# Cross-attention probabilities made by key instead of transposed, in a fused decoder layer

## The chip, the cores and the metric

One core of a Trainium2 chip runs the whole kernel. The metric is the device time of one execution in microseconds.

## The reference

A decoder layer over 32 independent batches of 112 tokens of width 256. The change touches only the cross-attention to 375 context positions, 16 heads of width 16:

```python
x = layernorm(x + self_attention_with_threshold(x, W))
q, k, v = heads(x @ Wq + bq), heads(ctx @ Wk + bk), heads(ctx @ Wv + bv)
scores = einsum('bhqd,bhkd->bhqk', q, k) / 4
scores = where(mask, -1e15, scores)            # mask depends on batch and key
attn = softmax(scores)                         # over the 375 keys
x = layernorm(x + einsum('bhqk,bhkd->bhqd', attn, v) @ Wo + bo)
x = layernorm(x + mixture_of_2_of_8_experts(x))
```

## The kernel before

All engines run one loop over iterations, and each iteration works on five batches at once, one per stage: in iteration `it` the stage "self" (self-attention) handles batch it+2, "proj" (q, k and v) it+1, "attn" (cross-attention scores to weighted values) it, "join" (output projection, second layer norm, gating) it-1, "moe" it-2. An iteration is cut into 20 slots (`SLOTS`). Every engine has its own in-order program that goes through the slots 0 to 19, and the engines meet only at semaphores. `USES` says in which slot TensorE makes each product of the other stages and in which PSUM bank (G0 to G2 or O); before a product, TensorE waits until the bank's previous product has been taken.

Batch a's cross-attention before: `scores(a, n)` on TensorE makes the 112 x 375 scores of one head as one fp32r matmul (q and k are split in a high and a low part, stacked on 96 partitions in `q_stack` and `k_stack`, which SP's DMA queue fills with 24 transfers a batch). The sign is turned, so the most negative value is the maximum. `head` on VectorE (L595) adds the mask, writes `masked` and gives the least value as `nmax`. `exponent` on ScalarE (L475) makes `probs` with `nmax` as bias and sums them. `transpose_probs` (L920) transposes them in three pieces into PSUM, ScalarE (L505) copies them to `probsT`, and `weigh_values` (L936) multiplies four heads at a time by the values into bank O. In the next iteration ScalarE copies the result to `o_sb` (L490), TensorE transposes the widened reciprocals (`rb`, L993), and VectorE multiplies them (`attnT`, L649) ahead of `Wo` (L1000).

Order within a slot on TensorE: first a score, then the transposes of an earlier head, then the slot's products, then, in slots 7, 11, 15 and 19, the weighing of values. Scores 0 and 1 of the next batch are in slots 18 and 19. Other names: `x1T`, `qT` (L968), `K0`, `K1` (L979), `V0` to `V2` (L986) are proj's products, `m0` to `m3` (L1042) the experts' (six fp32r matmuls of 512 columns each), `Sc`, `PT`, `att` self's, `x2T` and `lg` (L1030, L1033) join's. ScalarE takes `x1T` first in slot 0 (L484), `q_sb` in slot 3, `k_hi` (L528) in 4 and 7, `self_exp` (L519) in 6. SP's loop is: load x, context and mask, store the output, wait for `q_lo` from VectorE (slot 5), 12 transfers to `q_stack` (L386), 12 to `k_stack` (L395).

## Time and profile before

| what | us |
|---|---|
| median of 3 runs (868.3 to 870.01) | 868.95 |
| profiled execution, its own time | 868.0 |
| its span | 866.2 |
| TensorE busy | 829.0 (96%) |
| VectorE busy | 723.7 (84%) |
| ScalarE busy | 650.5 (75%) |
| GpSimd busy | 199.7 (23%) |

Matmul records overlap, since they are pipelined; busy time is the union of an engine's records. A line number names the instruction's line in the kernel before.

### The profile page before, as it was taken

To read this page: it belongs to the slowest core of one execution; us is meant where nothing else is said; L and a number is where in the kernel's file an instruction comes from. 1 tells how busy PE (TensorE), PEld (TensorE's weight loads), DVE (VectorE), ACT (ScalarE), POOL (GpSimd) and SP (SyncE) were. 2 spreads that over 40 slices of the span, in tenths; PEclk is the share of its full clock that TensorE was granted. 3 is DMA by queue.
4 is the path that set the end of the run, shared out by engine and by line. 5 is a ranking of instruction groups with operands and counts; after the bars stand their busy time and mean duration, and the time that the engine had idled before them with its cause. 6 is when DMAs were issued, how large, how long until landed. Compare 5 with 4: busy or idle time off the path is not lost.

```text
span 866.2 us, 25528 instructions
## 1 busy us (share of the span) xinstructions
PE 829.0 (96%) x7844; PEld 723.8 (84%) x7844; DVE 723.7 (84%) x2836; ACT 650.5 (75%) x1961; POOL 199.7 (23%) x293
## 2 busy tenths in 40 slices
PE   4789999999999999999999999999999999999985
PEld 3678888888888888888888888888888888888863
DVE  3547888888998888888988898998888998888765
ACT  2458877788887777888877788887777888777760
POOL 2202122222222222222222212222222222222101
PEclk9999999999999999999999999999999999999999
DMA  8634444443434444433444433444444333433300
GB/s 261 163 98 104 114 108 109 123 114 86 104 98 111 109 115 117 95 98 96 113 109 110 123 94 101 100 106 106 113 118 103 99 100 100 108 86 84 92 8 11
DMA packets 89830, 91.08 MB, mean 105 GB/s; under 512 B 19440, under 2 KB 85600, under 8 KB 89696
## 3 DMA queue, kind: packets, MB, share of 16 engines
q1 hardware_dynamic: 89696, 89.45, 41.0%
q8 instruction: 65, 1.06, 0.5%
q14 instruction: 69, 0.57, 0.2%
HBM read 26.84 MB, written 3.67 MB: 35 GB/s over the span
## 4 chain that ended last, share of the span: by engine, by line
PE 87%; DVE 3%; SPq 3%; DMA 2%; issue 2%; ACT 1%; POOL 1%; DVEq 0%; POOLq 0%; ACTq 0%
PE psum L1042 19%; PE psum L920 18%; PE psum L911 11%; PE psum L936 10%; PE psum L986 8%; PE psum L979 7%; PE psum L968 3%; PE psum L1000 3%; SPq L386 2%; SPq L395 1%; PE psum L957 1%; DVE mix L609 1%; PE psum L950 1%; PE psum L962 1%; DMA wout_sb<-in_wout 1%
## 5 line engine op out<-in xcount | busy, mean ns | idle before, releaser
L475 ACT ACTIVATE probs<-masked,nmax 112x375 f32<-112x375 f32 x512 | 312.9, 611 | 77.6 <-DVE nmax L595 76.6
L595 DVE CUSTOM_DVE_ANT_0 masked<-psum,mask_add 112x375 f32<-112x375 f32 x512 | 276.6, 541 | 53.7 <-PE psum L911 42.8
L505 ACT ACTIVATE probsT<-psum 125x336 f32<-125x336 f32 x512 | 228.6, 447 | 63.2 <-PE psum L920 58.3
L920 PE MATMUL psum<-const_sb,probs 112*125 112x112 f32 x1536 | 251.1, 272 | 0.1
L920 PEld LDWEIGHTS psum<-const_sb,probs 112*125 112x125 f32 x1536 | 235.8, 188 | 16.0 <-issue 6.8
L911 PE MATMUL psum<-k_stack,q_stack 96*112 96x376 f32 x512 | 203.4, 397 | 3.3 <-DMA k_stack<-k_hi 2.7
L418 POOL TENSOR_SCALAR var_eps<-moments 112x1 f32<-112x1 f32 x96 | 21.2, 220 | 485.6 <-DVE moments L699 191.1
L609 DVE SCALAR_TENSOR_TENSOR mix<-psum,gate,mix 112x256 f32<-112x256 f32 x224 | 107.7, 481 | 14.6 <-PE psum L1042 1.3
L1042 PE MATMUL psum<-we_hi,x_hi 128*112 128x512 f32 x256 | 108.0, 422 | 2.4 <-DVE mix L609 2.4
L911 PEld LDWEIGHTS psum<-k_stack,q_stack 96*112 96x112 f32 x512 | 90.1, 176 | 22.5 <-issue 13.4
L1042 PE MATMUL psum<-we_hi,x_lo 128*112 128x512 f32 x256 | 100.8, 394 | 0.0
L936 PE MATMUL psum<-probsT,v_sb 125*32 125x112 f32 x3072 | 100.1, 263 | 0.5 <-ACT probsT L505 0.5
L1042 PE MATMUL psum<-we_lo,x_hi 128*112 128x512 f32 x256 | 100.4, 392 | 0.0
L475 ACT ACTIVATION_READ_ACCUMULATOR probs<-masked,nmax 112x1 f32 x512 | 100.1, 196 | 0.0
L936 PEld LDWEIGHTS psum<-probsT,v_sb 125*32 125x32 f32 x3072 | 69.2, 109 | 19.5 <-issue 6.3
L452 POOL TENSOR_TENSOR ctx_lo<-ctx_sb,ctx_hi 128x752 fp32r<-128x752 f32 x32 | 57.9, 1809 | 118.3 <-DVE vac_scaled L739 107.4
L986 PE MATMUL psum<-wv_hi,ctx_hi 128*125 128x256 f32 x192 | 59.9, 312 | 1.5 <-DVE we_lo L577 0.9
L1042 PEld LDWEIGHTS psum<-we_hi,x_lo 128*112 128x112 f32 x256 | 44.7, 175 | 14.7
L422 POOL TENSOR_TENSOR rstd<-var_eps,minus_half 112x1 f32<-112x1 f32 x96 | 54.7, 569 | 8.0
L986 PE MATMUL psum<-wv_lo,ctx_hi 128*125 128x256 f32 x192 | 53.8, 280 | 0.0
L1042 PEld LDWEIGHTS psum<-we_hi,x_hi 128*112 128x112 f32 x256 | 45.0, 176 | 10.6 <-DVE mix L609 3.2
L986 PE MATMUL psum<-wv_hi,ctx_lo 128*125 128x256 f32 x192 | 53.8, 280 | 0.0
...
## 6 DMA issues: line engine op xcount, KB each, us to landing
k_stack<-k_hi SPq DMA_DIRECT2D x256, 93.8 KB, 2.2
q_stack<-q_hi SPq DMA_DIRECT2D x256, 56.0 KB, 2.0
...
k_stack<-k_lo SPq DMA_DIRECT2D x128, 93.8 KB, 2.2
q_stack<-q_lo SPq DMA_DIRECT2D x128, 56.0 KB, 2.0
...
```

Of the source, the lines that this page charges most:

```text
L422: nc.gpsimd.tensor_tensor(rstd[n - 1][:, :], var_eps[n - 1][:, :], minus_half[:, :], ALU.pow)\
L452: nc.gpsimd.tensor_tensor(ctx_lo[k][:, :, :], ctx_sb[k][:, :, :], ctx_hi[k][:, :, :].bitcast(fp32), ALU.subtract)\
L475: nc.scalar.activation(probs[:, n % RING, :], masked[:, n % RING, :], ACT.Exp, bias=nmax[:, n:n + 1], scale=-1.0, accum_out=probs_sum[a[1] ...
L505: nc.scalar.activation(probsT[:, i % TRING, :], psum[0:KP, T_BANKS[i % 2], 0:KT * TOK], ACT.Copy).then_inc(probsT_copied, 1)
L595: nc.vector.tensor_tensor_reduce(masked[:, n % RING, :], psum[0:TOK, S_BANKS[n % 2], 0:KEYS], mask_add[k][:, :], 1.0, 3.0e38, ALU.add, ALU ...
L609: nc.vector.scalar_tensor_tensor(out=mix[:, :], in0=bank_of[f"m{e // 2}"][0:TOK, (e % 2) * DIM:(e % 2 + 1) * DIM], scalar=gate[k][:, e:e + ...
L911: nc.tensor.matmul(psum[0:TOK, S_BANKS[n % 2], 0:KEYS_EVEN], q_stack[k][:, c, pair, odd, :], k_stack[k][:, c, pair, :], start=True, stop=T ...
L920: mm = nc.tensor.transpose(psum[0:KP, T_BANKS[n % 2], j * TOK:(j + 1) * TOK], probs[:, n % RING, j * KP:(j + 1) * KP], ident[0:TOK, 0:TOK])
L936: mm = nc.tensor.matmul(o_bank[32 * j:32 * j + 32, c * TOK:(c + 1) * TOK], v_sb[k][:, t, pair, odd:odd + 2, :].rearrange("p e d -> p (e d) ...
L979: mm = nc.tensor.matmul(bank[:, 0:KEYS_EVEN], w_part[:, c, r * 128:(r + 1) * 128], x_part[:, c, :], start=(n == 0), stop=(n == 3 * DC - 1))
L986: mm = nc.tensor.matmul(bank[0:KP, 0:DIM], x_part[:, c, j * KP:(j + 1) * KP], w_part[:, c, :], start=(n == 0), stop=(n == 3 * DC - 1))
L1042: mm = nc.tensor.matmul(bank[0:TOK, 0:width], x_part[:, c, :], w_part[:, c, :], start=(n == 0), stop=(n == len(parts) - 1))
```

## The change

The cross-attention is split over two stages and the scores are made twice. In "attn" (batch it) TensorE still makes the scores by query and VectorE still takes the least value, but only that value is used. After eight heads TensorE transposes the eight columns (`mx0`, `mx1`), ScalarE copies them negated into `nmaxT`, and SP sends them through a scratch tensor in DRAM to partition 96 of `q_stack`, whose partner row in `k_stack` is all ones. In the new stage "heads" (batch it-1) there are 12 blocks: ScalarE lays the mask of 125 keys by 4 x 112 queries into PSUM (`lay_mask`), TensorE adds two fp32r matmuls of 97 rows on top (`score_block`), and ScalarE's exponential writes the transposed probabilities at once (`exponent`). The values have a 17th column of ones, which gives the sum of the probabilities. The result is copied (`o_sb`), transposed to queries (`oT`), divided by VectorE (`rden`, `o_norm`), and transposed back (`aT`). "join" and "moe" move one iteration later, so that the loop has one iteration more. `q_stack`, `k_stack` and `v_sb` have three buffers, the mask has four. ScalarE's `ctx_hi` moves from slot 1 to slot 12, `V0` from 9 to 10.

```diff
+BLOCKS = QUADS * KT
+STACKS = 3
+MASKS = 4
...
-S_BANKS, T_BANKS, O_BANK, G_BANKS = (0, 1), (2, 3), 4, (5, 6, 7)
...
-USES = [("x1T", 0, "G2"), ("m0", 1, "G1"), ("rb", 1, "O"), ("qT", 2, "G2"), ("K0", 3, "G0"), ("Wo", 4, "G1"), ("Sc", 5, "G2"),
-        ("K1", 6, "G1"), ("m1", 8, "G0"), ("V0", 9, "G2"), ("x2T", 10, "G1"), ("PT", 11, "G0"),
-        ("m2", 12, "G2"), ("att", 13, "G1"), ("lg", 14, "G0"), ("V1", 15, "G2"), ("m3", 16, "G1"),
-        ("V2", 18, "G0")]
+S_BANKS, ST_BANKS, O_BANK, G_BANKS = (0, 1), (2, 3), 4, (5, 6, 7)
+USES = [("x1T", 0, "G2"), ("m0", 1, "G1"), ("aT", 1, "G0"), ("qT", 2, "G2"), ("K0", 3, "G0"), ("Wo", 4, "G1"),
+        ("Sc", 5, "G2"), ("K1", 6, "G1"), ("m1", 8, "G0"), ("mx0", 8, "G2"), ("V0", 10, "G2"), ("x2T", 10, "G1"),
+        ("PT", 11, "G0"), ("m2", 12, "G2"), ("att", 13, "G1"), ("lg", 14, "G0"), ("V1", 15, "G2"), ("oT", 15, "O"),
+        ("m3", 16, "G1"), ("mx1", 16, "G0"), ("V2", 18, "G0")]
...
-          "attn": (0, ()),
-          "join": (-1, ("rb", "Wo", "x2T", "lg")),
-          "moe": (-2, ("m0", "m1", "m2", "m3")),
+          "attn": (0, ("mx0", "mx1")),
+          "heads": (-1, ("oT",)),
+          "join": (-2, ("aT", "Wo", "x2T", "lg")),
+          "moe": (-3, ("m0", "m1", "m2", "m3")),
...
-FIRST, LAST = -2, BATCH + 2
+FIRST, LAST = -2, BATCH + 3
...
+            def neg_max_to_scratch(at, c):
+                sp.wait_ge(act_attn.sem, act_attn.to(f"nmaxT{c}", at))
...
+                sp.dma_start(neg_max_scratch[c], nmaxT[c][:, :].bitcast(fp32)).then_inc(neg_max_out[c], 16)
+            def neg_max_to_stack(at, c):
...
+                sp.wait_ge(neg_max_out[c], 16 * (at[1] + 1))
+                settle(sp)
+                sp.dma_start(q_stack[b][96:97, c, :, :, :].rearrange("o p h q -> o (p h q)").bitcast(fp32),
+                             neg_max_scratch[c].rearrange("(o h) q -> o (h q)", o=1)).then_inc(neg_max_in[b][c], 16)
...
+                if heads:
+                    neg_max_to_scratch(w, 1)
...
+                if heads:
+                    neg_max_to_stack(w, 1)
...
+                if attn:
+                    neg_max_to_scratch(a, 0)
...
+                        if n == 2 and attn:
+                            neg_max_to_stack(a, 0)
...
+                def lay_mask(w, i):
+                    b = w[1] % MASKS
+                    if i == 0:
+                        act.wait_ge(mask_in[b], turn(w, 1, MASKS))
+                        if w[1] == 0:
+                            act.wait_ge(setup_pe, 2)
+                    if due(count(w, BLOCKS, i - 1)):
+                        act.wait_ge(probs_ready, count(w, BLOCKS, i - 1))
+                    t = i % KT
+                    nc.scalar.activation(
+                        psum[0:KP, ST_BANKS[i % 2], 0:4 * TOK].rearrange("p (h q) -> p h q", h=4),
+                        mask_u8[b][:, KEYS + t * TOK:KEYS + (t + 1) * TOK].unsqueeze(1).broadcast_to([KP, 4, TOK]),
+                        ACT.Copy, scale=BIG).then_inc(mask_laid, 1)
+                def exponent(i):
+                    group, t = i // KT, i % KT
+                    act.wait_ge(blocks_ready, count(w, BLOCKS, i + 1))
+                    if t == 0 and due(count(w, QUADS, group - 1)):
+                        act.wait_ge(pv_done, count(w, QUADS, group - 1))
+                    nc.scalar.activation(probsT[:, group % 2, t, :], psum[0:KP, ST_BANKS[i % 2], 0:4 * TOK],
+                                         ACT.Exp, scale=-1.0).then_inc(probs_ready, 1)
...
+                    if heads and n < BLOCKS:
+                        exponent(n)
+                        if n + 2 < BLOCKS:
+                            lay_mask(w, n + 2)
+                    if n >= SLOTS - 2 and active("heads", it + 1):
+                        lay_mask(a, n - (SLOTS - 2))
+                    if join and n == 2:
+                        act.wait_ge(pe_join.sem, pe_join.to("aT", o))
+                        nc.scalar.activation(attnT[:, :], bank_of["aT"][:, 0:DC * TOK], ACT.Copy)\
+                          .then_inc(act_join.did("attnT"), 1)
+                    if attn and n in (9, 17):
+                        c = (n - 9) // 8
+                        act.wait_ge(pe_attn.sem, pe_attn.to(f"mx{c}", a))
+                        if due(16 * a[1]):
+                            act.wait_ge(neg_max_out[c], 16 * a[1])
+                        nc.scalar.activation(nmaxT[c][:, :], bank_of[f"mx{c}"][0:CHUNK_HEADS, 0:TOK],
+                                             ACT.Copy, scale=-1.0).then_inc(act_attn.did(f"nmaxT{c}"), 1)
...
+                    if heads and n == 14:
+                        act.wait_ge(pv_done, count(w, QUADS, QUADS))
+                        nc.scalar.activation(o_sb[:, :], o_bank[:, 0:QUADS * TOK], ACT.Copy)\
+                          .then_inc(act_heads.did("o_sb"), 1)
+                    if own and n == 12:
                         act.wait_ge(ctx_in[k], turn(s, 1))
...
+            for k in range(STACKS):
+                nc.vector.memset(v_sb[k][:, :, :, HEAD_DIM:HEAD_DIM + 1], 1.0)
+                nc.vector.memset(k_stack[k][0:96, :, :, KEYS:KEYS_EVEN].bitcast(fp32), 0.0)
+                nc.vector.memset(k_stack[k][96:97, :, :, :].bitcast(fp32), 1.0)
+            nc.vector.memset(o_bank[:, 0:QUADS * TOK], 0.0)
             nc.vector.memset(ones[:, :], 1.0).then_inc(setup_dve, 1)
...
                     nc.vector.tensor_tensor_reduce(
-                        masked[:, n % RING, :], psum[0:TOK, S_BANKS[n % 2], 0:KEYS],
+                        scores_left[:, n % 2, :], psum[0:TOK, S_BANKS[n % 2], 0:KEYS],
                         mask_add[k][:, :], 1.0, 3.0e38, ALU.add, ALU.min,
-                        nmax[:, n:n + 1]).then_inc(masked_ready, 1)
+                        nmax[:, h:h + 1]).then_inc(max_ready, 1)
...
+                            by_head = o_bank[0:TOK, :].rearrange("q (h r) -> q h r", h=HEADS)
+                            nc.vector.reciprocal(rden[:, :, :], by_head[:, :, HEAD_DIM:HEAD_DIM + 1])\
+                              .then_inc(dve_heads.did("rden"), 1)
+                            dve.wait_ge(dve_heads.sem, dve_heads.to("rden", w))
+                            nc.vector.tensor_tensor(
+                                o_norm[:, :, :], by_head[:, :, 0:HEAD_DIM],
+                                rden[:, :, :].broadcast_to([TOK, HEADS, HEAD_DIM]), ALU.mult)\
+                              .then_inc(dve_heads.did("o_norm"), 1)
...
+            def open_blocks():
+                for bank in ST_BANKS:
+                    for j in range(4):
+                        mm = nc.tensor.matmul(psum[:, bank, j * TOK:(j + 1) * TOK], ident, ident[:, 0:TOK],
+                                              start=(j == 0), stop=True, skip_group_check=True)
...
+                def score_block(w, i):
+                    b, group, t = w[1] % STACKS, i // KT, i % KT
+                    c = group // 2
+                    if i % (BLOCKS // DC) == 0:
+                        pe.wait_ge(neg_max_in[b][c], turn(w, 1, STACKS))
+                    pe.wait_ge(mask_laid, count(w, BLOCKS, i + 1))
+                    for e in range(2):
+                        pair = 2 * (group % 2) + e
+                        mm = nc.tensor.matmul(psum[0:KP, ST_BANKS[i % 2], 2 * e * TOK:2 * (e + 1) * TOK],
+                                              k_stack[b][:, c, pair, t * KP:(t + 1) * KP],
+                                              q_stack[b][:, c, pair, :, :].rearrange("p h q -> p (h q)"),
+                                              start=False, stop=True, skip_group_check=True)
+                    mm.then_inc(blocks_ready, 1)
+                def weigh_values(group):
...
+                    pe.wait_ge(probs_ready, count(w, BLOCKS, KT * group + KT))
+                    if group == 0:
+                        pe.wait_ge(dve_proj.sem, dve_proj.to("v2", w))
+                        if due(dve_heads.to("o_norm", o)):
...
+                            pe.wait_ge(dve_heads.sem, dve_heads.to("o_norm", o))
                     for t in range(KT):
                         for j in range(4):
-                            pair = 4 * c + j
                             mm = nc.tensor.matmul(
-                                o_bank[32 * j:32 * j + 32, c * TOK:(c + 1) * TOK],
-                                v_sb[k][:, t, pair, odd:odd + 2, :].rearrange("p e d -> p (e d)"),
-                                probsT[:, (4 * quad + j) % TRING, t * TOK:(t + 1) * TOK],
-                                start=(odd == 0 and t == 0), stop=(odd == 1 and t == KT - 1),
+                                o_bank[32 * j:32 * j + HEAD_DIM + 1, group * TOK:(group + 1) * TOK],
+                                v_sb[w[1] % STACKS][:, t, 4 * group + j, :],
+                                probsT[:, group % 2, t, j * TOK:(j + 1) * TOK],
...
                                 tile_position=(0, 32 * j), skip_group_check=True)
                     mm.then_inc(pv_done, 1)
...
                                                   w_part[:, c, :], start=(n == 0), stop=(n == 3 * DC - 1))
-                    elif name == "rb":
-                        pe.wait_ge(dve_attn.sem, dve_attn.to("rden_wide", o))
-                        pe.wait_ge(act_join.sem, act_join.to("o_sb", o))
+                    elif name in ("mx0", "mx1"):
+                        c = int(name[2])
+                        pe.wait_ge(max_ready, count(a, HEADS, CHUNK_HEADS * (c + 1)))
+                        mm = nc.tensor.transpose(bank[0:CHUNK_HEADS, 0:TOK],
+                                                 nmax[:, CHUNK_HEADS * c:CHUNK_HEADS * (c + 1)], ident[0:TOK, 0:TOK])
+                    elif name == "oT":
+                        pe.wait_ge(act_heads.sem, act_heads.to("o_sb", w))
+                        for g in range(QUADS):
+                            mm = nc.tensor.transpose(bank[0:TOK, g * 128:(g + 1) * 128],
+                                                     o_sb[:, g * TOK:(g + 1) * TOK], ident)
+                    elif name == "aT":
+                        pe.wait_ge(dve_heads.sem, dve_heads.to("o_norm", o))
                         for c in range(DC):
                             mm = nc.tensor.transpose(
...
-                    if attn and 2 <= n < HEADS + 2:
-                        transpose_probs(n - 2)
+                    if heads and n < BLOCKS - 1:
+                        score_block(w, n + 1)
+                    if n == SLOTS - 1 and active("heads", it + 1):
+                        score_block(a, 0)
                     for u, (name, slot, _) in enumerate(ALL_USES):
...
+                        open_blocks()
+                    if heads and n >= 4 and (n - 4) % 3 == 0 and n <= 13:
+                        weigh_values((n - 4) // 3)
                 if it == FIRST:
```

## Rows read from the trace of the kernel before

**Rows 1.** The page: busy time of each engine.

```profile
PE 829.0 (96%) x7844; PEld 723.8 (84%) x7844; DVE 723.7 (84%) x2836; ACT 650.5 (75%) x1961; POOL 199.7 (23%) x293
```

**Rows 2.** Windows, one iteration: length, PE, PEld, DVE, ACT, POOL busy, clock, DMA.

```profile
420.13:445.08 24.95, 24.95 (x244) 22.02 (x243) 22.24 (x88) 20.14 (x62) 6.16 (x10) 1.00 0.43 109
```

**Rows 3.** Chain of one iteration: shares, then pieces (start, us, line).

```profile
by line: PE psum L1042 22.3%; PE psum L920 21.5%; PE psum L911 12.6%; PE psum L936 11.4%; PE psum L986 9.1%; PE psum L979 8.3%; PE psum L968 3.6%; PE psum L1000 3.5%; PE psum L957 1.7%; PE psum L950 1.6%; PE psum L962 1.4%; PE psum L993 0.8
...
420.29 0.20 PE psum L993 x2
...
437.30 0.10 PE psum L1033
...
443.68 0.17 PE psum L911
443.85 1.40 PE psum L1042 x6
```

**Rows 4.** Groups by form, ScalarE: shapes, count, busy us and mean ns, idle before.

```profile
L475 ACT ACTIVATE probs<-masked,nmax 112x375 f32<-112x375 f32 x512 | 312.9, 611 | 77.6 <-DVE nmax L595 76.6
...
L505 ACT ACTIVATE probsT<-psum 125x336 f32<-125x336 f32 x512 | 228.6, 447 | 63.2 <-PE psum L920 58.3
...
L528 ACT ACTIVATE k_hi<-psum,bk_col 128x375 fp32r<-128x375 f32 x64 | 36.2, 566 | 2.0 <-PE psum L979 2.0
...
L484 ACT ACTIVATE x1T<-psum 128x224 f32<-128x224 f32 x32 | 11.2, 351 | 7.1 <-PE psum L962 6.8
```

**Rows 5.** Timeline of ScalarE at slot 0: start, duration.

```profile
443.72 0.36 ACT L484 ACTIVATE x1T<-psum 128x224 f32<-128x224 f32 x1
443.97 0.35 ACT L490 ACTIVATE o_sb<-psum 128x224 f32<-128x224 f32 x1
```

**Rows 6.** Timeline of TensorE: slot 0's x1T, slot 2's score 3.

```profile
443.27 0.41 PE L962 MATMUL psum<-const_sb,x 112*128 112x112 f32 x2
...
445.21 0.40 PE L911 MATMUL psum<-k_stack,q_stack 96*112 96x376 f32 x1
```

**Rows 7.** Timeline of VectorE: the end of head 1, then out_sb.

```profile
444.88 0.08 DVE L595 DVE_READ_ACCUMULATOR2_ANT nmax<- 112x1 f32 x1
445.48 0.41 DVE L642 TENSOR_SCALAR out_sb<-mix,moments,rstd 112x256 f32<-112x256 f32 x1 [0.52 <-POOL rstd L422]
```

**Rows 8.** Waits from 100 to 796 us: total, times, longest.

```profile
DVE masked L595 <- PE psum L911: 21.3, 48, 0.6
```

**Rows 9.** SP's queue: timeline, and the issues' time to landing.

```profile
450.41 0.59 SPq L386 DMA_DIRECT2D q_stack<-q_hi  x1
...
550.72 1.25 SPq L386 DMA_DIRECT2D q_stack<-q_hi  x2
...
566.71 1.27 SPq L395 DMA_DIRECT2D k_stack<-k_hi  x1
...
k_stack<-k_hi SPq DMA_DIRECT2D x256, 93.8 KB, 2.2
```

**Rows 10.** Timelines of VectorE and ScalarE at the start.

```profile
1.33 0.38 DVE L561 MEMSET v_sb<- 125x384 f32 x1
...
1.73 0.15 DVE L563 MEMSET ones<- 128x112 f32 x1
...
7.71 0.34 ACT L519 ACTIVATE self_exp<-psum,self_nmax 112x112 f32<-112x112 f32 x1
```

**Rows 11.** Timeline of TensorE: rb in iterations 2, 30, 31 and 32.

```profile
94.89 0.35 PE L993 MATMUL psum<-const_sb,rden_wide 112*128 112x112 f32 x2
...
796.02 0.36 PE L993 MATMUL psum<-const_sb,rden_wide 112*128 112x112 f32 x2
...
820.61 0.36 PE L993 MATMUL psum<-const_sb,rden_wide 112*128 112x112 f32 x2
...
841.59 0.36 PE L993 MATMUL psum<-const_sb,rden_wide 112*128 112x112 f32 x2
```

**Rows 12.** Windows of 2 us, TensorE in the drain: busy, clock, DMA.

```profile
852.00:854.00 2.00, 0.10 (x1) 1.00 0.00 0
```

284 lines of the change are left out of this document (123 added, 161 removed).

## The prediction

> **What bounds the kernel now.** I read the page first: TensorE is busy for 96% of the span [rows 1]. Then the windows view over exactly one turn of the loop, from one set of rb transposes to the next: 24.95 us, of which TensorE is busy for all, VectorE for 22.24, ScalarE for 20.14, at a granted clock of 1.00, which is 2.4 GHz [rows 2]. So TensorE sets the pace and VectorE is close behind. The chain through that turn is TensorE alone, and its shares say what each product costs [rows 3]: the transposes of the probabilities (L920) 21.5%, or 5.36 us; the scores (L911) 12.6%; m0 to m3 (L1042) 1.40 each; K (8.3%) 1.04 each; V (9.1%) 0.72 each; qT 0.89; Wo 0.87; weigh_values (11.4%) 0.71 each. The average turn over 28 of them is (796.02 - 94.89) / 28 = 25.04 us [rows 11], 0.09 above that clean turn.
>
> What the average hides is the order. TensorE, ScalarE and VectorE each walk through 20 slots in program order, and the question for each new hand-over is what stands in front of it.
>
> **TensorE's own work.** Removed: 5.36 us. Added: 12 blocks of two fp32r matmuls, 125 columns loaded and 224 streamed. In the chain, fp32r products pay by columns: 512 cost 1.40 / 6 = 0.233, 376 cost 0.17 [rows 3]. The slope puts 224 at 0.10, and one that streams only 8 still costs 0.10 (L1033) [rows 3], a floor for loading. So 0.105 each, 0.21 a block, 2.52 a turn. oT is four transposes, each 0.10 like those of rb (0.20 for two), 0.42 with the change of mode after it; mx0 and mx1 one each, 0.17 with it. aT replaces rb at the same price; weigh_values has as many matmuls as before. Sum: 24.95 - 5.36 + 2.52 + 0.42 + 0.34 = 22.87, call it 22.9 us. If that were all, the turn would be 2.05 us shorter.
>
> **ScalarE's own work.** Removed: 16 x (611 + 447) ns = 16.9 us of records (L475, L505) [rows 4], and the reads of the accumulator. Added: 12 exponentials and 12 masks of 448 columns. From 224 to 336 columns a copy grows from 351 to 447 ns, 0.857 ns a column [rows 4]. The exponential: 611 + 73 x 0.857 = 674 ns by L475, 566 + 63 = 629 by L528, which also reads PSUM; I take 0.65. The mask: 447 + 96 = 543 by L505; no row writes PSUM or reads bytes, so 0.45 to 0.60, and I take 0.56. In total 14.5 us, so ScalarE's busy time falls by some 3 us. The Trainium skill ("ScalarE: Activation LUTs", section What ACT_TABLE_LOAD costs) gives 280 ns + 0.833 a column with a pointer for the bias and 186 ns without: the first would be 0.65 for the exponential, the second 0.56 for it and for the mask; by the second the turn below would be 24.55 and the run some 6 us shorter. Where the two differ, L475 (611) lies nearer the first.
>
> **The new wait.** lay_mask(n+2) waits for exponent(n), the instruction just ahead of it, so these two don't overlap. And TensorE's block 2 stands in slot 1, ahead of m0, and needs lay_mask(2), which ScalarE issues in slot 0 behind x1T's copy and exponent(0). x1T's copy needs TensorE's slot 0. From the start of x1T on TensorE: 0.41 until its end [rows 6], 0.04 hand-over (443.68 to 443.72) [rows 5, 6], 0.25 from one copy to the next [rows 5], 0.65, 0.04, 0.56, 0.04: block 2 starts at 1.99. TensorE has only x1T (0.20, as rb) and one score (0.17) [rows 3] before it. It stands for 1.6 us, each turn, with nothing that could cover it, for m0 is queued behind.
>
> From there ScalarE needs 0.65 + 0.04 + 0.56 - 0.10 = 1.15 a slot, nine slots 10.35, plus attnT 0.25 and q_sb's two copies 0.5 [rows 5], two k_hi 0.92 (566 ns less 0.1 of overlap [rows 4]), self_exp 0.34 [rows 10]: lay_mask(11) is done at 1.95 + 12.35 = 14.3. TensorE's slots 1 to 9 and the first score of slot 10 are 12.6 us (m0, aT, qT, K0, Wo, Sc, K1, m1, mx0, two weigh_values, scores and blocks): 14.6. So ScalarE keeps up barely, and I add 0.2. The turn is 22.9 + 1.6 + 0.2 = 24.7 us, with the 0.09 on top [rows 11] 24.8: a gain of 0.25 a turn, over 28 turns 7 us.
>
> **VectorE.** It loses a reciprocal, a widening copy and attnT and gains a reciprocal and a multiply of 256 columns (0.41 by out_sb [rows 7]): about even. Its head 1 ends at 444.96 and TensorE's score 3 starts at 445.21 [rows 6, 7]: 0.25 apart, and out_sb then waits 0.52 for POOL [rows 7]. In 28 turns it waits 21.3 us for scores, 0.76 a turn [rows 8]: without these, a turn of its own is 24.95 - 0.76 = 24.2. It doesn't set the pace at 24.8, but a faster TensorE would find it at 24.2 (and 22.24 if all its gaps were waits [rows 2]). TensorE's new pause in slot 1 gives it that time. So even if ScalarE's price were much lower, little more than 1 us a turn could be won.
>
> **SP's queue.** From score 3 (445.21) to the first q_stack issue (450.41) is 5.2 us, from there to the last k_stack issue 16.0 (550.72 to 566.71), landing 2.2 [rows 6, 9]: 23.4 us round, with score 3 of the next turn waiting at its end. Into this come neg_max_to_scratch(a, 0) and neg_max_to_stack(a, 0). A q_stack issue takes 0.59 [rows 9], and these have far fewer rows; two add 0.7 to 1.2 with their waits, and 0.3 goes with the transposes: 23.8 to 24.3. Covered by the turn of 24.7, by half a microsecond. The other two go into SP's idle time. The first half of the maxima is on its way some 2 us before block 0 needs it; the second leaves once out_dram has been issued, lands 2.2 us later, and block 6 is in slot 5: about 1 us to spare. ctx_hi's move and x1_bo's third buffer cost nothing; POOL has the time.
>
> **What is paid once.** (a) The pipeline is one stage deeper. The iteration inserted near the end has no attn and no proj: 12 x 1.15 + 1.0 on ScalarE, then oT and o_norm, 16.3 us. The one before it took 20.98 us (820.61 to 841.59) [rows 11] and falls to 22.9 - 6.4 (its missing products by the shares) [rows 3] + 1.6 = 18.1. Net +13.4. (b) Three memsets of one partition by 3008 elements: v_sb's 384 elements took 378 ns, 112 took 152 [rows 10], 0.83 ns an element, so 2.56 us each; with o_bank's VectorE is free at 9.9 us instead of 1.9, and self_exp, at 7.71 before [rows 10], starts at 10.35. open_blocks adds eight fp32 matmuls ahead of att. Together 3.5 us (bounds 1 and 6). (c) Two issues more in the first turn, where SP's queue is what is waited for: 1. Sum 17.9.
>
> **The sum.** The profiled execution took 868.0 us, its span 866.2; the median of the runs is 868.95, 0.95 higher. 868.0 - 7 + 17.9 = 878.9, as a median 880. A turn of 24.3 is the break-even point.
>
> **Rivals.**
> 1. Faster: ScalarE's pair is nearer 0.95 us, the pause of TensorE shrinks, and VectorE's 24.1 is the turn; with once-costs of 14: 28 x (24.1 + 0.09 - 25.04) = -24, so 859. For it: the unknown price of a write into PSUM. Against: 0.41 + 0.25 + 0.61 in the chain of the pause are rows. 0.17.
> 2. The change does all it says (22.9 a turn): 868.95 - 58 + 18 = 829. Against it VectorE's 24.2. 0.04.
> 3. Slower by more: a wait on the ScalarE or DMA path costs another 0.9 us, turn 25.6 (ScalarE's self-wait 0.1 dearer each time makes its nine slots 1 us longer; or the maxima for block 6 land late): 868.95 + 18 + 18 = 905. It decides once SP's loop passes 24.7 or ScalarE's slot 1.2 us. 0.14.
> 4. fp32r at 224 columns runs at the rate of fp32. Wo's two matmuls of 256 columns take 0.87 (3.5%) [rows 3], so 224 would take 0.38: 24 x 0.275 = 6.6 us a turn, some 1075 in all. No fp32r product of the trace streams between 17 and 255 columns. 0.08.
> 5. The pause lowers TensorE's clock. In the drain it stayed at 1.00 in a window with 0.10 us of work out of 2 [rows 12]. If m0, qT and K0 ran at half rate: 3.3 us a turn, 975. 0.03.
> The forecast's own case, turns of 24.4 to 25.1, 869 to 891: 0.54.
>
> **How the numbers follow.** No change within 0.2% (1.7 us, about what a measurement can tell) takes 0.06 from the lower edge of the forecast's case. Faster: rivals 1 and 2, 0.21. Slower: the rest, 0.73. The range 858 to 905 leaves out rivals 2, 4 and 5 and the tails of the others, some 0.18.
>
> **What would show it.** In the trace after: the block matmuls 0.105 apart (rival 4 if 0.38); TensorE idle some 1.6 us ahead of block 2 in slot 1, released by ScalarE's mask, 32 times; mask 0.56, exponential 0.65; VectorE's waits for scores not much smaller; score 3 not waiting for k_stack; block 6 not waiting for q_stack; three memsets of 2.56 at the start; one more iteration of 16 us at the end. The prediction is wrong if the pause is under 1 us or the turn is outside 24.4 to 25.1.

## The result, and the profile after

The changed kernel takes 919.68 us (median of four runs, 918.96 to 923.61) against 869.13 for the kernel before: a ratio of 1.059, with a 95% interval of 1.056 to 1.062. The forecast was 880 with a range of 858 to 905. The sign was right; the size was short by 40 us, and the time lies outside the range.

The page of the changed kernel, its busy row and the row of TensorE's granted clock in 40 slices. TensorE's busy time fell from 829.0 us [rows 1] to 809.1, ScalarE's from 650.5 to 558.6, and the run still became longer.

```profile
PE 809.1 (88%) x7284; PEld 662.8 (72%) x7284; DVE 750.5 (82%) x2810; ACT 558.6 (61%) x1289; POOL 200.3 (22%) x293
...
PEclk9888799999999999999999999999999999999998
```

The same page's groups: shapes, count, busy us and mean ns, idle before. These are the three new instructions. The two of ScalarE cost less than forecast: exponential 0.536 (0.65 forecast), mask 0.543 (0.56). The third is the block's matmul; its 281 ns are the length of a record and not what it adds to TensorE's work, which is read further down from start to start.

```profile
L524 ACT ACTIVATE probsT<-psum 125x448 f32<-125x448 f32 x384 | 205.9, 536 | 24.3 <-PE psum L982 22.8
L513 ACT ACTIVATE psum<-mask_u 125x448 f32<-125x448 uint8 x384 | 206.8, 543 | 10.1
L982 PE MATMUL psum<-q_stack,k_stack 97*125 97x224 f32 x768 | 147.8, 281 | 13.5 <-ACT psum L513 12.3
```

Where the time went is read from the same instruction in each iteration. Timelines of TensorE: x1T of the iterations -1, 2 and 30, then aT of the iterations 31, 32 and 33.

```profile
21.72 0.61 PE L1024 MATMUL psum<-const_sb,x 112*128 112x112 f32 x2 [3.00 <-DVE x L855]
...
100.62 0.39 PE L1024 MATMUL psum<-const_sb,x 112*128 112x112 f32 x1
...
825.38 0.36 PE L1024 MATMUL psum<-const_sb,x 112*128 112x112 f32 x2
...
853.00 0.35 PE L1063 MATMUL psum<-const_sb,o_norm 112*128 112x112 f32 x2
...
874.38 0.36 PE L1063 MATMUL psum<-const_sb,o_norm 112*128 112x112 f32 x2
...
892.47 0.35 PE L1063 MATMUL psum<-const_sb,o_norm 112*128 112x112 f32 x2
```

In the kernel before, x1T stood at 92.35 in iteration 2 and at 794.20 in iteration 30, and its span was 866.2. So the 51.7 us between the spans are:

| stretch | before | after | difference | forecast |
|---|---|---|---|---|
| to x1T of iteration 2 | 92.35 | 100.62 | +8.3 | +4.5 |
| 28 turns | 25.07 each | 25.88 each | +22.9 | -7 |
| from there to the end | 72.0 | 92.5 | +20.5 | +13.4 |

The forecast's differences add up to 10.9 us, so 40.8 us of the 51.7 are the miss, and three quarters of it (29.9) are the turn. The mean of 25.88 holds two early turns, of the iterations 2 and 3, that took 26.10 and 28.09; all the others but one take 25.75 to 25.81. One turn after, in windows (length, PE, PEld, DVE, ACT, POOL busy, clock): TensorE is idle for 1.85 us of it, at a clock of 1.00, and VectorE is busy for 22.85 us where it was busy for 22.24 [rows 2].

```profile
438.35:464.16 25.81, 23.96 (x228) 19.78 (x227) 22.85 (x88) 17.23 (x40) 6.19 (x9) 1.00 0.42 106
```

The waits of TensorE, then of VectorE, from 200 to 700 us, which is 19.4 turns (total, times, longest). The mask (L513) that the forecast had made responsible for 1.6 us a turn is named for 0.26; VectorE is named for 1.45, in two places.

```profile
PE psum L968 <- DVE nmax L652: 16.2, 20, 0.8
PE psum L1048 <- DVE mix L666: 11.9, 20, 0.6
PE psum L982 <- ACT psum L513: 5.1, 20, 0.3
PE psum L1048 <- ACT nmaxT L550: 3.4, 20, 0.2
...
DVE scores_left L652 <- PE psum L968: 16.9, 47, 0.7
DVE out_sb L699 <- POOL rstd L456: 11.0, 20, 0.6
DVE x L855 <- POOL rstd L456: 8.0, 20, 0.4
```

The pause itself, in the timelines of TensorE, ScalarE and VectorE. From x1T to block 2 it is 1.82 us (1.99 forecast). But a first part of it, 0.82 us, is score 2 waiting for VectorE's head 0, and only then comes 0.24 for the mask. Head 0 ends at 439.38, and score 2 stands between it and block 2, so that by this chain block 2 could start 0.24 us before it does; the mask ends at 440.12.

```profile
438.35 0.36 PE L1024 MATMUL psum<-const_sb,x 112*128 112x112 f32 x2
439.53 0.40 PE L968 MATMUL psum<-k_stack,q_stack 96*112 96x376 f32 x1 [0.82 <-DVE nmax L652]
440.17 0.47 PE L982 MATMUL psum<-q_stack,k_stack 97*125 97x224 f32 x2 [0.24 <-ACT psum L513]
...
438.75 0.36 ACT L532 ACTIVATE x1T<-psum 128x224 f32<-128x224 f32 x1 [0.98 <-PE psum L1024]
439.00 0.54 ACT L524 ACTIVATE probsT<-psum 125x448 f32<-125x448 f32 x1
439.57 0.55 ACT L513 ACTIVATE psum<-mask_u 125x448 f32<-125x448 uint8 x1
...
439.30 0.08 DVE L652 DVE_READ_ACCUMULATOR2_ANT nmax<- 112x1 f32 x1
```

### The profile page after: what moved, and what is told of

Its sections match the earlier page's. It is cut to its first block, busy times and chain, and to the rows that moved or that the text cites. A ratio compares the mean times of both kernels' runs of the same rounds, so it can differ in the third digit from the quotient of the medians.

```text
span 917.9 us, 22878 instructions
## 1 busy us (share of the span) xinstructions
PE 809.1 (88%) x7284; PEld 662.8 (72%) x7284; DVE 750.5 (82%) x2810; ACT 558.6 (61%) x1289; POOL 200.3 (22%) x293
## 4 chain that ended last, share of the span: by engine, by line
PE 56%; DVE 21%; issue 10%; ACT 5%; SPq 5%; DMA 2%; POOL 0%; DVEq 0%; POOLq 0%; ACTq 0%
PE psum L1112 11%; PE psum L982 8%; DVE scores_left L652 7%; PE psum L1041 7%; PE psum L968 7%; PE psum L1048 6%; PE psum L998 5%; DVE mix L666 5%; PE psum L1030 3%; PE psum L1070 3%; SPq L413 2%; ACT psum L513 2%; ACT probsT L524 2%; SPq L427 2%; PE psum L1058 1%
## 5 line engine op out<-in xcount | busy, mean ns | idle before, releaser
L652 DVE CUSTOM_DVE_ANT_0 scores_left<-psum,mask_add 112x375 f32<-112x375 f32 x512 | 275.3, 543 | 70.9 <-PE psum L968 62.9
L968 PE MATMUL psum<-k_stack,q_stack 96*112 96x376 f32 x512 | 197.4, 394 | 32.0 <-DVE nmax L652 25.0
L524 ACT ACTIVATE probsT<-psum 125x448 f32<-125x448 f32 x384 | 205.9, 536 | 24.3 <-PE psum L982 22.8
L513 ACT ACTIVATE psum<-mask_u 125x448 f32<-125x448 uint8 x384 | 206.8, 543 | 10.1
L982 PE MATMUL psum<-q_stack,k_stack 97*125 97x224 f32 x768 | 147.8, 281 | 13.5 <-ACT psum L513 12.3
L982 PEld LDWEIGHTS psum<-q_stack,k_stack 97*125 97x125 f32 x768 | 131.8, 191 | 25.9 <-ACT psum L513 22.8
L666 DVE SCALAR_TENSOR_TENSOR mix<-psum,gate,mix 112x256 f32<-112x256 f32 x224 | 107.4, 479 | 18.1 <-PE psum L1112 6.0
L998 PE MATMUL psum<-probsT,v_sb 125*17 125x112 f32 x3072 | 98.5, 261 | 0.0
L998 PEld LDWEIGHTS psum<-probsT,v_sb 125*17 125x17 f32 x3072 | 66.0, 97 | 30.0 <-issue 21.0
L1048 PE MATMUL psum<-wv_hi,ctx_hi 128*125 128x256 f32 x192 | 60.7, 316 | 22.9 <-DVE mix L666 16.9
L555 ACT ACTIVATE o_sb<-psum 128x448 f32<-128x448 f32 x32 | 17.4, 544 | 77.1 <-PE psum L998 77.1
L1048 PEld LDWEIGHTS psum<-wv_hi,ctx_hi 128*125 128x125 f32 x192 | 35.6, 186 | 33.3 <-DVE mix L666 19.4
```

The costliest lines, as they stand in the source:

```text
L513: nc.scalar.activation(psum[0:KP, ST_BANKS[i % 2], 0:4 * TOK].rearrange("p (h q) -> p h q", h=4), mask_u8[b][:, KEYS + t * TOK:KEYS + (t + ...
L524: nc.scalar.activation(probsT[:, group % 2, t, :], psum[0:KP, ST_BANKS[i % 2], 0:4 * TOK], ACT.Exp, scale=-1.0).then_inc(probs_ready, 1)
L652: nc.vector.tensor_tensor_reduce(scores_left[:, n % 2, :], psum[0:TOK, S_BANKS[n % 2], 0:KEYS], mask_add[k][:, :], 1.0, 3.0e38, ALU.add, A ...
L666: nc.vector.scalar_tensor_tensor(out=mix[:, :], in0=bank_of[f"m{e // 2}"][0:TOK, (e % 2) * DIM:(e % 2 + 1) * DIM], scalar=gate[1 - k][:, e ...
L968: nc.tensor.matmul(psum[0:TOK, S_BANKS[n % 2], 0:KEYS_EVEN], q_stack[b][0:96, c, pair, odd, :], k_stack[b][0:96, c, pair, :], start=True, ...
L982: mm = nc.tensor.matmul(psum[0:KP, ST_BANKS[i % 2], 2 * e * TOK:2 * (e + 1) * TOK], k_stack[b][:, c, pair, t * KP:(t + 1) * KP], q_stack[b ...
```

## The experiments

"Turn" below is the mean of ten iterations in the middle, from x1T of iteration 10 to that of iteration 20: 25.06 before, 25.78 after. "Theory A" is the forecast's own, "B" that VectorE sets the pace, "B2" that two chains end together in slot 1, "C" that the memsets and `open_blocks` make the start longer, and "D" that SP's queue holds the turn up. Ratios are against the kernel before.

| run | median us | ratio, 95% interval | turn |
|---|---|---|---|
| e1: mask first | 907.25 | 1.045 (1.039 to 1.051) | 25.33 |
| e2: ctx_lo after x_cas | 902.98 | 1.040 (1.034 to 1.045) | 25.19 |
| e3: head 0 first | 920.61 | 1.059 (1.053 to 1.064) | 25.79 |
| e4: start | 913.89 | 1.052 (1.047 to 1.057) | 25.82 |
| e5: e1 and e3 | 908.49 | 1.046 (1.043 to 1.049) | 25.31 |
| e6: e5 and e2 | 894.21 | 1.029 (1.023 to 1.036) | 24.81 |
| e7: e6 and e4 | 887.25 | 1.022 (1.019 to 1.025) | 24.78 |
| e8: e7, maxima by ScalarE's queue | 885.94 | 1.022 (1.017 to 1.026) | 24.84 |
| e9: e8, mask early | 878.13 | 1.012 (1.008 to 1.016) | 24.80 |
| e10: e9, o_norm last | 887.76 | 1.023 (1.019 to 1.027) | 25.04 |
| e11: e9, no wait for GpSimd | 870.44 | 1.001 (0.999 to 1.003) | 24.45 |
| e12: e11, k by ScalarE's queue | 866.87 | 0.997 (0.996 to 0.998) | 24.47 |
| e13: ctx_hi back | 905.35 | 1.043 (1.039 to 1.047) | 25.29 |
| e14: m3 light | 939.67 | 1.080 (1.074 to 1.085) | 26.55 |
| e15: m1 light | 920.41 | 1.059 (1.054 to 1.064) | 25.79 |

**One part at a time.**

e1, on ScalarE:

```diff
+                    if heads and n == 0:
+                        exponent(0)
+                        lay_mask(w, 2)
                     if proj and n == 0:
...
-                    if heads and n < BLOCKS:
+                    if heads and 0 < n < BLOCKS:
```

> ScalarE takes exponent(0) and lay_mask(2) ahead of the copy of x1T in slot 0, so that block 2 finds its mask laid. Theory A (the prediction's: ScalarE's hand-over in slot 1 is what TensorE stands for, and its pause sets the turn): the whole pause of some 1.06 us between x1T and block 2 goes, the turn falls from 25.8 to 24.8, the run from 920 to about 890. Theory B (each turn has two parts, one paced by TensorE up to score 9, one paced by VectorE from its head 9 to head 0 of the next batch; the pause waits for VectorE's head 0, then only 0.24 us for the mask): only the 0.24 us of the mask go, 28 x 0.24 = 7 us, 913, and score 2 still waits 0.8 us for VectorE.

It gave 0.45 us a turn: neither the whole pause nor the 0.24 alone, so both figures missed. Why it is more than the 0.24 isn't shown. The waits of TensorE in this run no longer name the mask, and score 2 waits for head 0 as long as before (16.3 us, 20 times).

e2, on GpSimd:

```diff
-                    pool.wait_ge(dve_self.sem, dve_self.to("vac_scaled", s))
+                    pool.wait_ge(dve_self.sem, dve_self.to("x_cas", s))
```

> GpSimd's ctx_lo waits for VectorE's x_cas, so that the two don't run at once. Theory A: VectorE does not set the turn, no change, 920. Theory B: x_cas falls from 1.22 us to 0.48 in the part of the turn that VectorE paces; the turn falls by 0.5 to 0.75, the run to 899 to 906, and TensorE's V1 no longer waits 0.6 us for VectorE's e5. Should ctx_lo slow another instruction of VectorE in place of x_cas, the gain is smaller and that instruction shows it.

0.59 us a turn, 17 us in the run, as theory B had it. The wait of V1 for `mix` (11.9 us) is gone. The timelines of VectorE and GpSimd in the changed kernel, then the view of x_cas's line (minimum, median and longest ns) in the kernel before, in this run and in e13:

```profile
456.75 1.22 DVE L807 SCALAR_TENSOR_TENSOR x_cas<-w_sum,vac_scaled,x_sb 112x256 f32<-112x256 f32 x1
...
455.88 1.80 POOL L486 TENSOR_TENSOR ctx_lo<-ctx_sb,ctx_hi 128x752 fp32r<-128x752 f32 x1 [3.11 <-ACT sparseT L587]
```

```profile
L757 DVE SCALAR_TENSOR_TENSOR x_cas<-w_sum,vac_scaled,x_sb x32: 466/728/740, 11.7 to 785.7; 112x256 f32<-112x256 f32 x32
```

```profile
L807 DVE SCALAR_TENSOR_TENSOR x_cas<-w_sum,vac_scaled,x_sb x32: 465/466/485, 16.1 to 800.0; 112x256 f32<-112x256 f32 x32
```

```profile
L807 DVE SCALAR_TENSOR_TENSOR x_cas<-w_sum,vac_scaled,x_sb x32: 462/704/881, 16.1 to 801.8; 112x256 f32<-112x256 f32 x32
```

x_cas takes 0.466 us alone and 1.216 (median) in the changed kernel, where it starts about half-way through GpSimd's ctx_lo. In the kernel before it already met the last 0.45 us of ctx_lo and took 0.728. In nearly every turn of both kernels, and of e13, it ends 0.28 us behind the end of ctx_lo, wherever it started: it was held up until ctx_lo was done. So the change cost VectorE 0.49 us a turn here (1.216 against 0.728). x_cas reads both w_sum and x_sb from SBUF. The Trainium skill ("GPSIMD Engine Reference", Key points) says that GpSimd shares its SBUF interfaces with VectorE and contends with VectorE instructions that have two SBUF inputs; the rows agree (0.466 against 1.216).

e13, the undoing of the moved step alone:

```diff
-            ("self", ["self_exp", "ctx_hi", "sparseT"]),
+            ("self", ["ctx_hi", "self_exp", "sparseT"]),
...
-                    if own and n == 12:
+                    if own and n == 1:
                         act.wait_ge(ctx_in[k], turn(s, 1))
```

> The changed kernel with ctx_hi back in ScalarE's slot 1, as before the change; nothing else. If the move of ctx_hi is what makes GpSimd's ctx_lo run beside x_cas for longer: x_cas falls from 1.16 us to 0.69, the turn by 0.45 to 25.3, the run to 907. Against it: 0.75 us of ScalarE's time come back into the slots in which it lays a mask for each block; then blocks 3 to 6 wait for the mask, up to 0.7 us a turn, and the sum is 0 to +7 us.

x_cas falls to 0.704, the turn to 25.29, the run to 905, and the waits for masks don't grow (5.1 us, 20 times). The run met its forecast. ctx_hi's place was free on ScalarE either way; its move cost 0.5 us a turn on VectorE, 14 of the 40 us.

e3, on VectorE:

```diff
                     if n == 18:
+                        if active("attn", it + 1):
+                            head(p, 0)
...
-                        if active("attn", it + 1):
-                            head(p, 0)
```

> VectorE takes head 0 of the next batch first in slot 18, ahead of o_norm and the experts 6 and 7; its total work stays. Theory A: the mask for block 2 is ready at the same time as before, so the pause keeps its end: at most 0.1 us a turn, 917 to 920. Theory B: the chain from head 9 now ends in expert 7, which m0 waits for behind block 2, instead of head 0, which score 2 waits for: 0.8 us of waiting for head 0 go, but the mask (L513) stands next at 0.25 us behind and expert 7 at 0.4: a gain of 0.2 to 0.5 us a turn, 906 to 914.

No gain, so theory B's figure missed here. The waits of TensorE, 200 to 700 us, show why: the time that score 2 no longer stands for head 0, block 2 stands for the mask.

```profile
PE psum L982 <- ACT psum L513: 23.7, 20, 1.3
PE psum L1048 <- DVE mix L666: 12.0, 20, 0.6
```

e5 makes the edits of e1 and e3 at once.

> The mask ahead of x1T's copy on ScalarE and head 0 first on VectorE, both at once. Theory B2 (behind x1T two chains of nearly the same length end, ScalarE's copy, exponential and mask at 1.8 us, and VectorE's head 0 at 1.2 us with score 2 and 0.24 us for it; taking one away leaves the other): each alone gave 0.45 and 0.0 us a turn, both give some 0.8 to 0.9, for m0 is next held by expert 7 at 1.3 us behind x1T: turn 24.9, 895. Theory A (ScalarE's pause alone): no more than the 0.45 us of the mask alone, turn 25.3, 907.

25.31, the same as e1 alone; theory A's number, theory B's missed. Block 2 still stands 0.57 us for its mask (10.2 us in 18 waits), since exponent(0) can't start ahead of block 0 in slot 19. Expert 7 comes later by the length of head 0, but m0, which needs it, stands behind block 2 and is named for no wait. Several chains end in slot 1, and taking one or two away leaves another.

e15 and e14 take the same 0.93 us of TensorE's work out of slot 8 or, with "m3" for "m1", out of slot 16; the products with the low parts are left out:

```diff
+                            if name == "m1":
+                                parts = [part for part in parts if part[1] is hi and part[2] is w_hi]
```

> The same cut in m1 (slot 8), in the part ahead of score 9. Theory A: again 24.9, 894, the same as for m3. Theory B (TensorE paces this part): VectorE's head 9 no longer waits 0.29 us and head 6 keeps its wait; the chain through VectorE then starts 0.3 us earlier, not 0.9: turn 25.4 to 25.5, 908 to 912.

> The changed kernel with m3 (slot 16) made of two matmuls instead of six: the products with the low parts are left out, 0.93 us less for TensorE in the part of the turn behind score 9. Theory A (TensorE's own work and the pause set the turn): turn 25.8 less 0.9, 24.9, the run 894. Theory B (VectorE paces that part): TensorE only waits longer for VectorE's head 0 and the mask; turn 25.6 to 25.8, 914 to 920.

m1's cut is worth nothing, which neither theory had. Its waits (200 to 700 us) show ScalarE in place of the work that left: 12.5 us in 39 waits for masks instead of 5.1 in 20. Slots 1 to 11 are paced by the pair exponential and mask, just as much as by TensorE.

```profile
PE psum L968 <- DVE nmax L652: 15.4, 19, 0.8
PE psum L982 <- ACT psum L513: 12.5, 39, 0.4
```

m3's cut makes the kernel slower, by 0.77 us a turn, which neither theory had either. TensorE stands 1.69 us for head 0 instead of 0.82, and in three turns of four it then works at half clock for a while. Two windows of 1 us, then a turn in which the clock fell and the next one, in which it didn't (length, PE, PEld, DVE, ACT, POOL busy, granted clock), and the timeline at 450.29:

```profile
449.00:450.00 1.00, 0.00 (x0) 0.00 (x0) 0.96 (x4) 0.97 (x3) 0.00 (x0) 1.00 0.58 135
...
452.00:453.00 1.00, 1.00 (x5) 0.76 (x4) 0.46 (x4) 0.09 (x1) 0.57 (x1) 0.50 0.99 322
...
448.25:475.12 26.87, 24.48 (x224) 20.50 (x223) 23.00 (x88) 17.22 (x40) 6.18 (x9) 0.94 0.42 105
475.12:500.41 25.29, 22.89 (x223) 19.06 (x222) 22.71 (x88) 17.13 (x40) 6.18 (x9) 1.00 0.42 105
```

```profile
450.29 0.40 PE L968 MATMUL psum<-k_stack,q_stack 96*112 96x376 f32 x1 [1.69 <-DVE nmax L652]
```

Three in four turns of this run are like the first (26.8 us); the others take 25.3 at a clock of 1.00, with the same wait of 1.70 for head 0. With 0.82 us in that place the changed kernel keeps 1.00. So at full clock 0.47 of the 0.93 us come back, where theory B had at most 0.2: TensorE waits 0.88 longer for head 0, and its waits for the mask of block 2 and for nmaxT (8.5 us of 500 in the changed kernel) are all but gone. The run bears out half of theory B, and it shows that a longer stand of TensorE can cost more than the work that was saved.

e4, the start:

```diff
-                nc.vector.memset(k_stack[k][96:97, :, :, :].bitcast(fp32), 1.0)
...
+                nc.gpsimd.memset(k_stack[k][96:97, :, :, :].bitcast(fp32), 1.0).then_inc(setup_pool, 1)
...
                         sum_attn_w()
-                        open_blocks()
+                    if it == FIRST and n == 13:
+                        open_blocks()
```

> The three memsets of one row of k_stack go from VectorE to GpSimd, and TensorE's opening of the score banks from before att to behind it, in the first iteration. Theory C (the start's 6.3 us are these two): x1T of iteration -1 starts at 15.5 to 16 instead of 21.7, and the run is 6 us shorter, 914. Rival: the transfers of the weights at the start end no earlier, so that the next wait (K0 or the split of the weights) takes the gain back: 918 to 920.

x1T of iteration -1 starts at 15.05, against 21.72 in the changed kernel and 15.40 before. The run is 5.8 us shorter: theory C holds. In the changed kernel's timelines of VectorE and TensorE the terms can be read: each memset 2.56 as forecast, with 0.67 of idle time ahead of it that was not, and the eight matmuls (sixteen records) of open_blocks, 2.73 us from their start to att's (L1019).

```profile
1.62 2.56 DVE L617 MEMSET k_stack<- 1x3008 f32 x1 [0.67 <-issue]
...
15.39 2.89 PE L951 MATMUL psum<-const_sb 128*128 128x112 f32 x16
18.12 0.60 PE L1019 MATMUL psum<-x_sb,sparseT 112*112 112x256 f32 x2
```

**Parts together, towards a kernel that wins.**

> The two edits of the run before and ctx_lo behind x_cas. Theory B (VectorE paces the second part of the turn): its 0.6 us add to the 0.9 of the other two, turn 24.3, 878. Rival (TensorE's own work is 24.0 to 24.5 a turn and is reached before): turn 24.4 to 24.6 with TensorE busy for over 97 of 100, 881 to 887.

e6 has the edits of e1, e2 and e3. 24.81 and 894.21 lie above what either theory gave, but e2's 0.5 us came on top of the others, as B had it.

> All four edits. The start gives its 6.5 us in full: 6.5 below the run before, 871 to 880. If the time of the first turns is set by loads or the clock and not by the start of x1T, less of it comes through.

7.0 us less, in full, though e6's four times lie as far apart as 889.36 and 900.56; the 871 to 880 were missed together with e6's figure.

e8 moves the four issues of the maxima to ScalarE (slots 9, 13, 17 and 1 of the next iteration):

```diff
-                sp.dma_start(neg_max_scratch[c], nmaxT[c][:, :].bitcast(fp32)).then_inc(neg_max_out[c], 16)
+                act.dma_start(neg_max_scratch[c], nmaxT[c][:, :].bitcast(fp32)).then_inc(neg_max_out[c], 16)
```

> As the run with all four edits (turn 24.73), but the four issues of the maxima go from SP's queue to ScalarE's. Theory D (SP's queue is the third chain that ends in slot 1: score 2 waits for pair 2 of k_stack, whose issue comes behind the maxima's two): SP's round loses 0.66 + 0.48 us, score 2 follows x1T at once, the turn falls to 24.3 to 24.5, the run from 887 to 876 to 881. Theory B (VectorE and the mask set the pace there by now): no more than 0.2 us a turn, over 882; the issues may cost ScalarE 0.3 us each and the mask comes later.

Theory D missed: in e7 score 2 had followed the landing of k_stack's pair 2 (three issues; the last, the first of the two recorded at 418.12, lands 2.2 us later, and score 2 starts at 420.37), that wait went (7.9 us to 0.5), and the turn didn't fall. SP's queue ended together with the others and did not set the pace.

```profile
415.75 0.35 SPq L348 DMA_DIRECT2D q_stack<-neg_max_scratch  x1
416.14 0.60 SPq L427 DMA_DIRECT2D k_stack<-k_hi  x1
416.79 1.29 SPq L427 DMA_DIRECT2D k_stack<-k_lo  x1
418.12 1.25 SPq L427 DMA_DIRECT2D k_stack<-k_hi  x2
...
420.37 0.40 PE L973 MATMUL psum<-k_stack,q_stack 96*112 96x376 f32 x1 [0.23 <-issue]
```

e9 frees the mask's chain altogether:

```diff
-        ("m3", 16, "G1"), ("mx1", 16, "G0"), ("V2", 18, "G0")]
+        ("m3", 16, "G1"), ("mx1", 16, "G2"), ("V2", 18, "G0")]
...
-                    if n >= SLOTS - 2 and active("heads", it + 1):
-                        lay_mask(a, n - (SLOTS - 2))
+                    if n in (13, 14) and active("heads", it + 1):
+                        lay_mask(a, n - 13)
...
-                    if n == SLOTS - 1 and active("heads", it + 1):
+                    if n == SLOTS - 2 and active("heads", it + 1):
                         score_block(a, 0)
```

> As the run with the maxima on ScalarE's queue, and: masks 0 and 1 of the next batch in ScalarE's slots 13 and 14, block 0 in TensorE's slot 18 instead of 19, mx1 in bank G2 so that V2 doesn't wait for its copy. If the hand-over of the mask is what is left: block 2 waits for nothing, V2's 0.17 us goes too, turn 24.0 to 24.2, 868 to 873. If VectorE's expert 7, which m0 waits for, is next: 24.2 to 24.4, 873 to 879.

The waits for masks fall to 2.0 us of 500 and those for nmaxT to none, and the turn stays at 24.80, above both figures: again the wait only moved, to m0, which stands 0.37 us for expert 7. The median of 878.13 lies in the second range, but not because of the turn; it is 7.8 us lower than e8's, while the two profiled spans differ by only 3.4, and the rest isn't explained.

e10 takes rden and o_norm after expert 7.

> As the run before, and VectorE divides (rden, o_norm) after expert 7 instead of ahead of the experts 6 and 7, so that m0 finds its bank free 0.65 us earlier. If VectorE is what m0 waits for in the run before: another 0.3 to 0.5 us a turn, 23.7 to 23.9, 860 to 867. If TensorE's own work is already all there is (24.0 or more a turn): no change against the run before.

A miss, and 10 us slower. m0 no longer waits, but score 3 then stands 0.82 us for head 1 (14.6 us in 500). From top_p to gate_a VectorE takes 2.07 us instead of 1.82, since top_i now stands right behind top_p, whose result it needs, with nothing between them: these 0.25 us match the 0.24 by which the turn grew. Reordering VectorE's work alone (e3, e5, e10) chose which consumer was late and never shortened the turn.

e11 takes away where VectorE itself stands still: out_sb behind head 2, rden and o_norm ahead of x1:

```diff
-                    if n == 1 and active("moe", it - 1):
+                    if n == 2 and active("moe", it - 1):
                         dve.wait_ge(pool_moe.sem, pool_moe.to("rstd3", shift(m, -1)))
...
+                        if heads:
+                            dve.wait_ge(pe_heads.sem, pe_heads.to("oT", w))
...
                         if own:
                             dve.wait_ge(pool_self.sem, pool_self.to("rstd1", s))
```

> As the run with the early mask (turn 24.78), and VectorE no longer stands for GpSimd: rden and o_norm go ahead of x1, which waited 0.40 us for rstd1, and out_sb goes behind head 2, which waited 0.55 for rstd3. Theory B (VectorE's own work and its two waits for GpSimd make the turn, TensorE has 24.1 of its own): VectorE's turn falls by 0.95 and TensorE's own is reached, 24.1 to 24.2, the run 859 to 863, below the kernel before the change. Theory D (the round of SP's queue, q_lo to k_stack to score 2 and back, is what holds it at 24.7 to 24.8 since three different edits ended there): no change, 876 to 880, and score 2 or 3 then waits for k_stack.

The 0.95 us of waits for GpSimd are gone and the turn falls by 0.35, the first edit since e6 that shortens it, as theory B had it in kind. It is a third of what was taken away, and the turn doesn't reach 24.1: VectorE then waits longer for scores (20.2 us of 500 instead of 13.0). The time can't be told from that of the kernel before.

e12 gives k_stack's last pair to ScalarE's queue:

```diff
-                    for n in range(PAIRS):
+                    for n in range(PAIRS - 1):
...
+                    if proj and n == 15:
...
+                            act.dma_start(k_stack[b][32 * third:32 * third + 32, :, last, 0:KEYS].bitcast(fp32),
```

> As the run before (turn 24.41, mean over 28 turns 24.63), and the three issues of k_stack's last pair go from SP's queue to ScalarE's, in slot 15, where it stands idle for 2 us. Theory D (the turns that are 0.3 to 2.4 us longer than the others, and the first ones, are those in which an issue of SP's queue took 0.5 to 1.2 us more and score 2 or 3 came late): SP's round falls by 1.9 us, the long turns go, the mean falls to 24.4 to 24.45, the run by 5 to 8 us to 863 to 866, below the kernel before the change. Rival (ScalarE's issues delay gate_exp or the maxima, or the long turns have another cause): 869 to 875.

866.87, just below the kernel before (0.997, 0.996 to 0.998); the gain of 3.6 us is less than the 5 to 8 expected. The turn in the middle is the same; the mean over 28 turns falls from 24.63 to 24.49. In the two profiles the two longest turns are 26.83 and 26.60 in e11 and 25.25 and 25.02 here, which is what theory D had of it. This is the best kernel of the study. Its page and its waits from 200 to 700 us:

```profile
PE 804.2 (93%) x7284; PEld 659.4 (76%) x7284; DVE 724.3 (84%) x2807; ACT 559.1 (65%) x1289; POOL 207.6 (24%) x296
```

```profile
PE psum L978 <- DVE nmax L662: 3.6, 19, 0.2
PE psum L978 <- issue: 2.2, 5, 0.6
PE psum L994 <- ACT psum L506: 1.5, 7, 0.4
```

Against the kernel before it wins 5.5 us at the start and 28 x 0.58 = 16 in the turns, and gives 20 back at the end.

## Why the prediction was wrong

**TensorE's own work: mis-sized by 1.1 us a turn.** The forecast took 24.95 down to 22.87. Summed from start to start over four turns (443.27 to 543.58 before, 438.35 to 541.47 after), without the waits, it is 25.08 and 23.94, a fall of 1.14 and not 2.08. Two terms make most of it: the transposes were 4.80 a turn from start to start, not the 5.36 that the chain's share gave, and the blocks are 2.84, not 2.52, for those next to m0, V2 or a weighing take 0.25 to 0.32 and not 0.21. The two matmuls of a block are 0.105 apart, as forecast, so rival 4 was false. In the forecast's own sum this term alone would explain the turn: 23.94 of work and 1.84 of waits make 25.78, and 1.8 of waits was forecast. But e15 takes 0.93 us of this work away and the turn stays, and e2 and e13 shorten it without touching TensorE. So the sum is not what sets the turn.

**ScalarE's chain: right.** The forecast put lay_mask(11) at 14.3 us after x1T and TensorE's need for it at 14.6; in the changed kernel the mask is done at 14.4 and block 11 starts at 14.5. The pause of 1.99 measured 1.82. By the Trainium skill's price without a pointer ("ScalarE: Activation LUTs", What ACT_TABLE_LOAD costs) both instructions would take 0.56; the rows have 0.536 and 0.543, so that price was the nearer one. It would have made the forecast 6 us lower, and so worse. As a cause the pause was overrated: head 0 fills 0.82 us of it, and e1, which takes the mask out of it, wins 0.45 us a turn, not 1.6.

**"VectorE: about even, a turn of its own of 24.2": the step that failed.** By the forecast's own count (turn less its waits for scores) the changed kernel's VectorE needs 25.78 - 16.9 / 19.4 = 24.9, and so it could not hide behind 24.8. The failed sentence is "ctx_hi's move and x1_bo's third buffer cost nothing; POOL has the time". GpSimd had the time, but the later ctx_hi put its ctx_lo on top of VectorE's x_cas. e13, which undoes only the move, gives back 0.49 us a turn, 14 of the 40 us; e2, which takes away the overlap that the kernel before had as well, gives 0.59, 17 us. At 0.49 the turn would still be 25.29, outside the forecast's 24.4 to 25.1, so this step is the largest that was found and not the whole.

**One sum for the turn: wrong in kind.** The forecast added the pause to TensorE's work. In fact the turn passes from one engine to the next. Up to score 9 TensorE and ScalarE's pairs pace it (e15: less work there, same turn, more waits for masks). Behind score 9 it is mostly VectorE: from there to the end of the turn it waits for scores about 0.2 us in all (heads 10 and 12), and TensorE waits for it twice (V1 and score 2). The weighings went from slots 7, 11, 15 and 19 to 4, 7, 10 and 13, and the blocks stand in slots 0 to 10, so that TensorE's work is early in the turn and VectorE's is late. In slot 1 the mask, head 0, expert 7 and k_stack's landing end within a microsecond of each other (e1, e3, e5, e7 to e9). This is why nothing taken alone gave what its wait in the list promised. What share of the turn's remaining 0.5 us (25.29 in e13 against 24.8) belongs to which of these wasn't separated.

**SP's queue: half a microsecond longer than forecast.** It took part in the tie at a turn of 24.8 (e7; 23.8 to 24.3 was forecast), and cost the turn nothing there (e8).

**The start: 3.5 forecast, 6.3 measured,** 0.3 outside the bounds of 1 and 6. The memsets' price was right; 3 x 0.67 of idle time ahead of them was left out, and open_blocks, for which the 3.5 leave 0.9, took 2.73. e4, which moves both, shows that together they are all of it. The other 2.0 us up to iteration 2 come with waits ahead of scores and blocks and with a lower granted clock in the filling pipeline, and so do the 2.6 us by which the turns of the iterations 2 and 3 exceed the steady ones. The windows below are the changed kernel from x1T of iteration -1 to that of iteration 2 and on to that of iteration 4, then two of 4 us at a clock of 0.50, then the same two stretches of the kernel before; behind the busy times stands the clock, 0.85 and 0.89 against 0.96 and 1.00. So what rival 5 feared did happen, but in the fill, and not by the pause in slot 1 alone. Whether the waits or the clock came first there wasn't tried.

```profile
21.72:100.62 78.90, 60.22 (x372) 50.63 (x373) 46.38 (x158) 29.36 (x66) 16.55 (x16) 0.85 0.45 120
100.62:154.81 54.19, 48.43 (x427) 39.98 (x427) 39.00 (x152) 34.64 (x80) 9.60 (x13) 0.89 0.40 100
...
100.00:104.00 4.00, 3.17 (x13) 2.22 (x12) 1.11 (x4) 2.71 (x6) 0.00 (x0) 0.50 0.58 135
104.00:108.00 4.00, 4.00 (x18) 4.00 (x18) 1.61 (x6) 3.30 (x9) 0.00 (x0) 0.50 0.48 163
```

```profile
15.40:92.35 76.95, 65.51 (x539) 57.14 (x540) 46.55 (x172) 46.75 (x135) 16.01 (x18) 0.96 0.51 136
92.35:143.17 50.82, 50.33 (x491) 44.13 (x487) 44.36 (x177) 40.77 (x123) 10.41 (x15) 1.00 0.45 112
```

**The end: +13.4 forecast, +20.5 measured.** The iteration before the inserted one went from 20.98 [rows 11] to 21.4, where 18.1 was forecast, and the inserted one took 18.1 and not 16.3. The first has 2.1 us of waits for masks and 0.8 for VectorE; the second 2.0 for masks and 1.6 for expert work. The rest is 2 us longer, 1.2 of it ahead of iteration 31. No edit shortened the stretch (92.0 to 95.3 us in all fifteen runs), and none was aimed at it: the cause is read, not shown.

**The rivals.** The outcome is nearest to rival 3, slower by more (a turn of 25.6, 905), but its mechanism, SP's or ScalarE's loop passing the turn, was not it. Slower had a chance of 0.73 and came; the range was too narrow above, because VectorE getting slower had no rival of its own.
